# Gated cross-attention layer: root steps of three norms on GpSimd, A's transfers at another place, the matmul shift for query pair 0 as well, and the next q product behind the whole context

## The reference

```
qh = softmax over the 64 head columns (Wq  @ layernorm(x))  * 64**-0.5     # 8 heads
kh = softmax over the 1024 positions  (Wk  @ ctx);   vh = Wv @ ctx
out = Wo @ (context(kh, vh) applied to qh) + bo
u   = out / max(|out| over the 128 channels, 1e-12) * g * sqrt(128)
x   = x + tanh(g_xattn) * u
scores = layernorm(x) @ Wr.T;  gates = softmax of the top 16 of 64, scattered
h   = layernorm(x) @ A (64 experts x rank 16);  y = (h * gates) @ B * 2
out = x + tanh(g_ffn) * y
```

## Time and profile before

| | |
|---|---|
| median of 3 runs | 977.32 us |
| profiled execution | 975.75 us, its span 974.1 us |
| mean granted TensorE clock | 0.992 |
| PE busy | 928.2 us (95%) |
| DVE, ACT, POOL busy | 708.3, 531.6, 464.9 us |
| moved by DMA | 88.30 MB, mean 91 GB/s |

### The profile page before, as it was taken

The page is one execution under the profiler, slowest core; times in us unless marked ns, Lnnn a source line. Parts: engine busy times, 40 slices in busy tenths (PEclk is TensorE's granted clock), DMA queues, the critical chain, the costliest instruction groups (busy, mean ns, idle before and its releaser), DMA issues.

```text
span 974.1 us, 16214 instructions
## 1 busy us (share of the span) xinstructions
PE 928.2 (95%) x5036; PEld 790.3 (81%) x5036; DVE 708.3 (73%) x1541; ACT 531.6 (55%) x1214; POOL 464.9 (48%) x311
## 2 busy tenths in 40 slices
PE   4899999999999999999989779999999999999998
PEld 3687777788887878787858679999999999999986
DVE  5888888878888888888897738766666666666621
ACT  5888887788878887887867624222222222222100
POOL 3665656677777867785757824311111111111100
PEclk9999999999999999999999989999999999999999
DMA  4216221232223122311311754111111111111001
GB/s 151 87 65 233 103 104 47 87 131 72 101 87 131 65 93 103 131 65 46 127 62 51 252 231 151 66 65 66 65 66 67 65 65 65 64 58 51 22 22 43
DMA packets 24805, 88.30 MB, mean 91 GB/s; under 512 B 3264, under 2 KB 3264, under 8 KB 24768
## 3 DMA queue, kind: packets, MB, share of 16 engines
q1 hardware_dynamic: 19296, 67.91, 19.1%
q0 software_dynamic: 5184, 19.40, 6.1%
q10 hardware_dynamic: 288, 0.52, 0.2%
HBM read 71.04 MB, written 16.78 MB: 90 GB/s over the span
## 4 chain that ended last, share of the span: by engine, by line
PE 64%; DVE 15%; ACT 10%; issue 8%; POOL 1%; DMA 1%; DVEq 0%; ACTq 0%; POOLq 0%
PE ps L60 18%; PE ps L62 18%; PE ps L61 18%; ACT qe L602 7%; PE ps L1284 3%; PE ps L1293 3%; DVE kmax L868 3%; DVE qT_lo L888 2%; DVE qtop L874 2%; DVE ekT_lo L895 2%; PE ps L1387 1%; PE ps L1358 1%; DVE mt L912 1%; DVE std_t L81 1%; ACT qT_hi L610 1%
## 5 line engine op out<-in xcount | busy, mean ns | idle before, releaser
L452 POOL TENSOR_TENSOR rb<-u_in,rb 128x1024 f32<-128x1024 f32 x14 | 33.7, 2408 | 260.1 <-DVE rb L864 260.1
L398 POOL TENSOR_TENSOR qe<-qe,qrec 128x1024 f32<-128x1024 f32 x64 | 121.3, 1905 | 54.5 <-DVE qrec L882 54.5
L60 PE MATMUL ps<-aT_hi,yT_hi 128*128 128x448 f32 (+2 forms) x384 | 128.2, 334 | 9.0 <-issue 9.0
L62 PE MATMUL ps<-aT_lo,yT_hi 128*128 128x448 f32 (+2 forms) x384 | 126.5, 329 | 0.0
L61 PE MATMUL ps<-aT_hi,yT_lo 128*128 128x448 f32 (+2 forms) x384 | 126.4, 329 | 0.0
L602 ACT ACTIVATE qe<-ps,qtop 128x64 f32<-128x64 f32 x512 | 111.3, 377 | 27.6 <-DVE qtop L874 27.6
L888 DVE TENSOR_TENSOR qT_lo<-ps,qT_hi 128x512 fp32r<-128x512 f32 x128 | 82.5, 686 | 51.8 <-ACT qT_hi L610 51.3
L391 POOL TENSOR_TENSOR qhalf<-qe 128x512 f32<-128x512 f32 x64 | 82.0, 1282 | 69.5 <-ACT qe L602 69.3
L60 PE MATMUL ps<-bT_hi,hT_hi 128*128 128x512 f32 x256 | 102.5, 400 | 0.0
L62 PE MATMUL ps<-bT_lo,hT_hi 128*128 128x512 f32 x256 | 99.9, 390 | 0.0
L61 PE MATMUL ps<-bT_hi,hT_lo 128*128 128x512 f32 x256 | 99.7, 390 | 0.0
(11 more groups left out here) (148 smaller groups left out, 2358.6 us busy)
## 6 DMA issues: line engine op xcount, KB each, us to landing
x_in<-in_x SPq DMA_DIRECT2D x16, 512.0 KB, 4.4
ctx_in<-in_ctx SPq DMA_DIRECT2D x16, 512.0 KB, 4.9
ctxT_in<-in_ctxT SPq DMA_DIRECT2D x16, 512.0 KB, 3.3
ctxT_hi<-in_ctxT POOLq DMA_DIRECT2D x16, 512.0 KB, 3.7
u_scratch<-osb SPq DMA_DIRECT2D x16, 512.0 KB, 3.8
out<-res SPq DMA_DIRECT2D x16, 512.0 KB, 2.8
x<-in_x SPq DMA_DIRECT2D x15, 512.0 KB, 3.9
u_in<-u_scratch SPq DMA_DIRECT2D x14, 512.0 KB, 3.2
```

The source lines that it names most:

```text
L60: nc.tensor.matmul(psum, whi, mhi, start=start, stop=False)
L62: return nc.tensor.matmul(psum, whi, mlo, start=False, stop=stop)
L398: nc.gpsimd.tensor_tensor(v, v, w, ALU.mult).then_inc(q_norm, 1)
```

## The change

Four things are changed.

1. `SHIFTED` is (0, 1, 2) instead of (1, 2): pair 0 too gets its maximum through two products on TensorE, and one exponential instead of 16. The argument that split pair 0's exponentials in two halves around `hi_kc` goes.
2. On TensorE both halves of `context(b-1)` stand together, and `mm_q(b,0)` behind them. On VectorE `max_q(b,0)` moves behind `sum_q(b-1,3)`, the first steps of the next layer norm and `lo_kc`.
3. Of `early_norms` VectorE keeps the clamp and the guess (`early_guess`); the three Newton steps are done by GpSimd in one block of 12 instructions (`early_newton`) in body 14, between `mt_lo` and `normalise(14, 0)`. GpSimd's loop ends one body earlier for it.
4. In GpSimd's body 15 all five last transfers of A stand behind `halve(15, 2)`, ahead of `add_first(1)`. Before, two stood behind `halve(15, 2)` and three in body 16.

```diff
-    SHIFTED = (1, 2)
+    SHIFTED = (0, 1, 2)
...
+            def early_newton():
+                s, r, t = ns[:, :, :], nr[:, :, :], nt[:, :, :]
+                pool.wait_ge(n_guess, 2)
+                for k in range(4 * NEWTON):
+                    if k > 0:
+                        pool.wait_ge(n_newton, k)
+                    if k % 4 == 0:
+                        last = nc.gpsimd.tensor_tensor(t, r, s, ALU.mult)
+                    elif k % 4 == 1:
+                        last = nc.gpsimd.tensor_tensor(t, t, r, ALU.mult)
+                    elif k % 4 == 2:
+                        last = nc.gpsimd.tensor_scalar(t, t, -0.5, 1.5, ALU.mult, ALU.add)
+                    else:
+                        last = nc.gpsimd.tensor_tensor(r, r, t, ALU.mult)
+                    last.then_inc(n_newton, 1)
...
-                if tail and not head:
-                    for t in range(5, DC):
-                        hi_a(t)
...
+                if isinstance(b, int) and b == NB - 2:
+                    early_newton()
                 if head and not ahead:
                     add_first(0)
...
-                if head and not ahead:
-                    add_first(1)
                 if head:
                     halve(b, 2)
                 if head and not ahead:
-                    for t in range(3, 5):
+                    for t in range(3, DC):
                         hi_a(t)
+                    add_first(1)
...
-                if head and started(b):
-                    exp_q(b, 0, (0,))
                 if tail:
                     hi_kc(b - 1)
...
-                    exp_q(b, 0, (1,) if started(b) else (0, 1))
+                    exp_q(b, 0)
...
-            def early_norms(steps):
+            def early_guess():
+                s, r = ns[:, :, :], nr[:, :, :]
+                dve.wait_ge(n_sum, 1)
+                nc.vector.tensor_scalar(s, psN_early.rearrange("p (e n) -> p e n", e=EARLY), MIN_SS, None,
+                                        ALU.max).then_inc(n_guess, 1)
+                dve.wait_ge(n_guess, 1)
+                first_root(r, s).then_inc(n_guess, 1)
```

More of the change, by code:

```diff
@@ L519, in _ @@
                 body(b, head=True, tail=True, ahead=True, split=True)
-            with pool.Fori(SPLIT + DC, NB - 1) as b:
+            with pool.Fori(SPLIT + DC, NB - 2) as b:
                 body(b, head=True, tail=True, ahead=True)
+            body(NB - 2, head=True, tail=True, ahead=True)
             body(NB - 1, head=True, tail=True, ahead=False)
@@ L598, in exp_q @@
                 act.wait_ge(q_max, 4 * b + p + 1)
-                for h in halves:
+                for h in range(2):
                     for n in range(H):
@@ L855, in norm_step, with spread @@
                 last.then_inc(n_step, 1)
-            def early_norms(steps):
[L858 to L863, removed]
+            def early_guess():
[5 more added lines that the diff above has]
+                first_root(r, s).then_inc(n_guess, 1)
+            def spread(slot, dst, *done):
+                dve.wait_ge(*done)
                 nc.vector.transpose(dst[:, :], nr[:, slot, :].unsqueeze(2).broadcast_to([P, N // 32, 32])).then_inc(n_spread, 1)
@@ L1040, in norm_u @@
             def norm_u(e):
-                before = NRT * (e - EARLY + 1)
+                before = NRT * (e - EARLY)
                 for k in range(NRT):
@@ L1045, in norm_u @@
                 dve.wait_ge(x2_done, e)
-                spread(0, rb, before + NRT)
+                spread(0, rb, n_step, before + NRT)
             stats(0)
@@ L1071, in body @@
                     dve.wait_ge(ctx_lo, 2 * NB)
-                    spread(0, rb_first[0], NRT)
+                    spread(0, rb_first[0], n_newton, 4 * NEWTON)
                 if ahead and started(b):
                     stats(b + 1)
+                if early:
+                    part_early(b - 2)
+                if norms:
+                    early_guess()
+                if ahead and started(b):
+                    std(b + 1, range(5))
+                if tail and head:
+                    sum_q(b - 1, 3)
+                if tail:
+                    lo_kc(b - 1)
+                if tail and not head:
+                    sum_q(b - 1, 3)
                 if head and started(b):
                     max_q(b, 0)
[L1077 to L1082, removed]
-                if norms:
-                    early_norms(range(2))
-                if tail:
-                    lo_kc(b - 1)
-                if head and started(b):
                     max_k(b, 1)
@@ L1110, in body @@
                     sum_q(b, 0)
-                if norms:
-                    early_norms(range(2, 4))
                 if tail:
@@ L1129, in body @@
                                                            ALU.mult, ALU.subtract).then_inc(fold_lo, 1)
-                if norms:
-                    early_norms(range(4, 7))
                 if tail and not head:
@@ L1134, in body @@
                     dve.wait_ge(q_T, 8 * NB)
-                    spread(2, rb, NRT)
+                    spread(2, rb, n_newton, 4 * NEWTON)
                 if tail:
@@ L1147, in body @@
                     lo_k(b, 2)
-                if norms:
-                    early_norms(range(7, 10))
                 if last:
@@ L1154, in body @@
                     lo_k(b, 3)
-                if norms:
-                    early_norms(range(10, NRT))
                 if last:
@@ L1314, in fold @@
                 if isinstance(b, int) and b == NB - 3:
-                    pe.wait_ge(n_step, 1)
+                    pe.wait_ge(n_guess, 1)
                 for j in range(CH):
@@ L1344, in sum_u @@
                 pe.wait_ge(n_part, e + 1)
-                pe.wait_ge(n_step, NRT * (e - EARLY + 1))
+                if not (isinstance(e, int) and e == EARLY):
+                    pe.wait_ge(n_step, NRT * (e - EARLY))
                 nc.tensor.matmul(psN, sel[:, :, :].rearrange("p q n -> p (q n)"), part[:, 0, :],
@@ L1417, in body @@
                     context(b - 1, 0)
+                    context(b - 1, 1)
                 if head:
@@ L1421, in body @@
                     mm_q(b, 0)
-                if tail:
-                    context(b - 1, 1)
-                if head:
                     mm_k(b, 1)
```

5 lines of the change are left out of this document (3 added, 2 removed).

## The result

The changed kernel takes 963.02 us (median of four runs, 961.49 to 963.50) against 977.39 for the kernel before in the same session: a ratio of 0.9854, 95% interval 0.9831 to 0.9876. That is 14.3 us less, where 10 to 11 were forecast. The profiled execution took 961.49, of which the span is 959.7.

What follows compares the result with a forecast made beforehand. TensorE, busy 95% of the span, was taken as the bound, so only its stalls could be recovered: -1.6 - 0.9 - 0.6 - 5.9 - 1.0 = -10.0 from 975.75, adjusted to 966.5 us; range 960.5 to 972.5.

Steps and rivals of the forecast that it cites:

- The forecast's own interval: Whole kernel: the time lands between 963.5 and 969.5 us; chance 0.55.
- the hand-over: Before feed-forward's `up(0,0)`: engines nearly full, so issuing A's transfers earlier closes only small gaps, -1.0 us (bounds 0 and -9).
- rival 1: Hand-over: A's transfers all land by 561, giving 5 us instead of 1, so 962.5; chance 0.12.
- Ordinary bodies and bodies 2 to 4: Attention loop: exponential wait goes, VectorE's chain runs earlier; 0.15 us less per ordinary body (-1.6), 0.3 in bodies 2 to 4 (-0.9).
- Rival 2: Loop: pair 0's late maximum makes its shift a new stall; at 1.0 us a body, 982; chance 0.07.
- rival 4: Loop: VectorE's earlier chain closes the 0.3 us hole and the one before `output`, 0.4 each: 962; chance 0.10.
- Start: Body 0: one exponential of 1.01 us replaces 16 taking 3.39, a quarter of the saving counted: -0.6 (0 to -2.4).
- Body 14: Twelve root steps on GpSimd take 5.4 us and remove body 14's 6.8 us loss, less 0.9 for lateness: -5.9.
- The 0.9 charged to TensorE for GpSimd's lateness: Body 14: GpSimd's later work starts 1.7 us late; `mm_k(b+1,0)` waits for `ctx_lo`, costing TensorE 0.9.
- The stated test: The prediction is wrong if bodies take over 33.5 us or the hole before `up(0,0)` is under 6 us.
- The fold's wait for `kc_lo`: Body 16: this wait shrinks too but lies inside the hand-over hole, so no gain was counted.

Runs made afterwards that it cites:

- experiment 3: Changed kernel with pair 0 back to 16 exponentials with bias, in one block, without its shift products: 968.50 us.
- experiment 4: Changed kernel with `mm_q(b,0)` again between the context's halves and its maximum back early on VectorE, pair 0's shift kept: 970.00 us.
- experiment 10: Kernel before with only the root steps on GpSimd and A's transfers at their new place; loop order and biases stay: 965.67 us.
- experiment 8: Changed kernel with `b_raw` loads waiting for A, A's first three issues ahead of `lo_c(15)` and `spread_first(1)`, and VectorE's root seed ahead of the statistics: 956.58 us.
- experiment 1: Changed kernel with the root's Newton steps given back to VectorE in the five groups of the kernel before: 971.46 us.
- experiment 7: Changed kernel with A's first three transfers issued ahead of `lo_c(15)` and `spread_first(1)` on GpSimd: 955.29 us.
- experiment 2: Changed kernel with A's last five transfers back at their old places and `add_first(1)` ahead of them: 964.01 us.
- experiment 9: Kernel before with only the loop's two edits; root steps stay on VectorE and A's transfers at their old places: 973.07 us.
- experiment 5: Changed kernel with SyncE's `b_raw` loads waiting until all eight of A's transfers have landed: 961.31 us.
- experiment 11: Changed kernel with A's first three issues ahead of `lo_c(15)` and `spread_first(1)`, and the other five ahead of `halve(15,2)`: 954.55 us.

## Why the prediction was right, and where it was not

The time, 963.02, is in the range (960.5 to 972.5) and 3.5 us under the point. The forecast's own interval began at 963.5. By the ledger the two traces are 14.4 us apart for 10.0 forecast, and almost all of the difference is one term, the hand-over; the slower start of `up` hid 0.97 of it. What came is close to rival 1 (chance 0.12, 962.5): A landed some 5 us earlier by the clock of fold 15, where the forecast had 1.

**Ordinary bodies and bodies 2 to 4: right, by its own steps.** From the context's first product, the shift starts at 8.41 (8.43 counted), the maximum on VectorE at 7.13 (345.75; 7.15 counted), `mm_q(b,1)` at 11.26 (11.3 counted). The 0.15 a body came as 0.14; of folds 1 to 5 the last three came as 0.39 to 0.50 for 0.3. It comes in two places: 0.05 up to `mm_q(b,1)`, and 0.10 from there to the transposes that wait for `ekT_lo` (5.93 after 6.03), though that wait itself stays in the trace. Rival 2, the shift as a new stall, did not happen. What I had not seen is that the margin is thin from another side: with only one of the two edits, a body is 0.35 to 0.38 us slower than with neither (experiments 3, 4, 10). The price of rival 4 was a slip of the sum: 0.4 in each of 14 bodies is 5.6 us instead of 2.5, which gives 963.4 and not 962.

**Start: -0.73 for -0.6.** The size of this is open: the first fold of the ten kernels whose start is the same lies anywhere from 47.7 to 49.7 us. The sign holds as far as the traces go, since the two kernels with the old start have 50.4 (before) and 51.3 (experiment 10).

**Body 14: right in mechanism, 0.8 too small.** The steps took 5.2 us for 5.4, with some luck: nine of the twelve took 0.39 each and not 0.3, and the next began 0.08 behind the end of the one before and not 0.15. The 0.9 charged to TensorE for GpSimd's lateness was not due: folds 14 to 15 take 32.63, less than an ordinary body, and no wait of TensorE there has GpSimd's late work as releaser. `ctx_lo` had the room. A part came back one body earlier, 0.36 us in folds 13 to 14: the seed, still on VectorE, met `halve` (experiment 8). By the Trainium skill ("GPSIMD Engine Reference", section 3.1 Elementwise) a two-input elementwise step costs GpSimd 1.96 times what it costs VectorE; the traces have 0.39 against 0.20 for the first one (`nt` from `nr` and `ns` at 488.88 of experiment 1), so they agree, though the same step at 498.01 took 0.26, a ratio of 1.5; and experiment 1 shows that the move pays all the same.

**Hand-over: the failed step.** I wrote that from 553 to 557 the GpSimd queue "already took 89% of the engines' time, so it ran nearly without a gap", and that "only small gaps go". The stated test, a hole not under 6 us, came out against it: 4.84. The queue was not full. In those 4 us, which begin with the issue of three transfers, it moved 1.11 MB at 89%; in 4 us behind the issue of five it moved 1.66 MB at 112%. Read as a rate against another stretch, and not as a share against 100%, has a third to spare. The number of transfers outstanding does not make the difference: three alone moved 0.82 MB in 2 us (536 to 538 of the changed kernel), and five moved 1.01 MB in 4 us in experiment 7. The low rates of these traces stand in the first microseconds behind an issue; what makes them low is open.

The whole 5.43 us from fold 15 to `up(0,0)` is not the placement's, though. A's landing ends this stretch. By the pair with experiment 2 (41.51), 4.14 are the placement and 1.29 the rest; in time the placement gave 1.8 to 2.8 (1.0 forecast), because of the clock. And traces with the same place of issue differ among themselves. With the last group issued 30.3 to 30.5 us behind fold 15 (before, experiments 2 and 9), A's last transfer landed 41.4 to 43.6 us behind it. With all five issued at 23.9 to 24.4 (the changed kernel, experiments 1, 4, 5 and 10), it landed 37.3 to 41.3 us behind, and the changed kernel's is the earliest. The means of the two groups are 3.1 us apart. So the direction is shown, and some 2 us of the 5.43 are a short tail that the next kernel may not have. The fold's wait for `kc_lo`, 1.1 us before, was rightly priced at nothing: it is gone in experiment 9 too, and the hole there is longer by more than that.

The Trainium skill's rule that each DMA engine takes turns between the two queues ("DMA: Bandwidth & Descriptors", section SWDGE vs HWDGE vs iDMA) does hold when they meet: in experiment 2 they moved 1.07 and 1.34 MB from 547 to 553. The change escapes most of it by having A nearly done at 548, when `b_raw` begins.

**The clock behind the hole** has no term in the prediction. The first 6 us of `up` ran at 0.50, the lower level (1.2 GHz), after 4.84 us in which TensorE did nothing. In the earlier trace rows the hole was longer and the products behind it were slow for a shorter time (10 of the first 24, against 16). This gave back 0.97 us, and experiments 7 and 11 win 2.8 us against the changed kernel by keeping the higher level.

What stays open: what sets the rate of the queue behind an issue and the length of its tail, and why the clock fell behind a hole of 2.30 us and not behind one of 2.86.

## What to carry to other kernels

A queue's share of the DMA engines' time says little about room: compare the bytes per microsecond with the best stretch of the same queue. Look for the place where the issuing engine waits for a transfer anyway: three issues put there were worth 4 us, more than the whole placement of the change. Do not take one trace for the length of a transfer's tail: with the same place of issue it moved the landing by up to 4 us. And price a set of edits of one loop together, since here each was a loss without the other.

## What the runs showed of the hardware

- GpSimd's queue moved 1.01 MB in the 4 us behind an issue of five transfers (535 to 539 in experiment 7) and 1.66 MB in 4 us later (543 to 547 in the changed kernel); three transfers alone moved 0.82 MB in 2 us (536 to 538 there).
- A batch of transfers on that queue ends with a tail of single packets, some 0.16 us apart with an idle hardware queue (experiment 5) and 0.33 beside a busy one (experiment 1). The last landing came 1.9 to 4.9 us behind the bulk.
- An integer pass of 128x96 on VectorE took 0.21 us alone and 1.31 beside GpSimd's 128x512 sum; a 128x96 step with three operands 0.26 and up to 2.33.
- The first 24 products of `up`, from start to start, took 4.74 us behind holes of 2.86 and 2.01 us, 6.35 behind one of 2.30, 7.53 behind 4.84 and 6.12 behind 8.99: the cost of a restart did not grow with the hole.
